# The opening of the forward scans in a convolution-attention, Mamba and expert block: gate projections swapped, state 2 and state 3 prepared in another order

## What is computed

```python
x = x + conv_attention(groupnorm(x))      # keeps the top tenth of each row of scores
t = tokens(x)
t = t + mamba_both_ways(layernorm(t))     # state-space scan, forward and backward
t = t + experts(layernorm(t))             # 8 experts, the best 2 for each token
```

```python
xs, z = split(x @ in_proj_w.T);  xs = silu(causal_conv(xs) + conv_b)
dbc = xs @ x_proj_w.T                     # 16 columns for dt, 16 of B, 16 of C
dt = softplus(dbc[:, :16] @ dt_proj_w.T + dt_proj_b)
h_s[t] = exp(dt[t] * A_s) * h_s[t-1] + dt[t] * B_s[t] * xs[t]    # 16 states s
y = sum over s of h_s * C_s + xs * D;   out = (y * silu(z)) @ out_proj_w.T
```

## Time and profile before

| | us |
|---|---|
| three timed runs: median (lowest to highest) | 1384.38 (1384.08 to 1384.41) |
| profiled execution | 1386.96 |
| its span, first to last instruction | 1385.2 |
| busy: PE, DVE, ACT, POOL | 1246.2, 1136.5, 1000.5, 840.9 |

### The profile page before, as it was taken

The page is one execution under the profiler, slowest core; times in us unless marked ns, Lnnn a source line. Parts: engine busy times, 40 slices in busy tenths (PEclk is TensorE's granted clock), DMA queues, the critical chain, the costliest instruction groups (busy, mean ns, idle before and its releaser), DMA issues. The chain is left out here.

```text
span 1385.2 us, 17997 instructions
## 1 busy us (share of the span) xinstructions
PE 1246.2 (90%) x4857; PEld 675.5 (49%) x4857; DVE 1136.5 (82%) x1352; ACT 1000.5 (72%) x1498; POOL 840.9 (61%) x450
## 2 busy tenths in 40 slices
PE   6249899999988999999989989999998899999969
PEld 2236355554537445455545635545453744545544
DVE  4876799997796689999688679999779668999952
ACT  3826889798755779799755688979865578979923
POOL 3112598797171389889345269879717138988932
PEclk9679899999999989999989979999999999999989
DMA  3000122221030012222021012222103011232203
GB/s 83 16 1 2 49 92 104 89 96 61 16 123 16 33 61 94 106 92 106 1 91 63 3 49 90 106 92 96 56 1 122 16 33 63 91 106 92 107 0 138
DMA packets 30641, 91.91 MB, mean 66 GB/s; under 512 B 4806, under 2 KB 8780, under 8 KB 30572
## 3 DMA queue, kind: packets, MB, share of 16 engines
q1 hardware_dynamic: 27836, 90.03, 18.5%
q10 hardware_dynamic: 2736, 1.08, 0.4%
HBM read 88.34 MB, written 2.75 MB: 66 GB/s over the span
## 5 line engine op out<-in xcount | busy, mean ns | idle before, releaser
L739 POOL TENSOR_TENSOR work<-expo,ring 128x1024 f32<-128x1024 f32 x128 | 300.4, 2368 | 101.2 <-DVE expo L1534 93.0
L739 POOL TENSOR_TENSOR ring<-ring 128x1024 f32<-128x1024 f32 x128 | 301.1, 2373 | 12.0 <-DVE ring L1534 12.0
L1534 DVE TENSOR_TENSOR_SCAN ring<-ring,ps 128x1024 f32<-128x1024 f32 x128 | 284.3, 2262 | 4.0 <-issue 2.1
L1534 DVE TENSOR_TENSOR_SCAN expo<-ring,ps 128x1024 f32<-128x1024 f32 x128 | 285.2, 2270 | 1.8 <-PE ps L1999 1.6
L2036 PE MATMUL ps<-work,ident 128*128 128x512 f32 x512 | 252.0, 598 | 0.8
L2036 PE MATMUL ps<-ring,ident 128*128 128x512 f32 x512 | 246.5, 603 | 3.7 <-POOL ring L739 3.0
L800 ACT ACTIVATE b_dtx_tok<-dtx_tok,b_tok 128x256 f32<-128x256 f32 x448 | 189.3, 493 | 0.0
L1053 ACT ACTIVATE ring<-dt_f,decay 128x1024 f32<-128x1024 f32 x128 | 147.0, 1149 | 42.6 <-DVE expo L1534 24.3
L2036 PEld LDWEIGHTS ps<-ring,ident 128*128 128x128 f32 x512 | 88.7, 190 | 110.9 <-issue 58.5
L1989 PEld LDWEIGHTS ps<-ident,b_dtx_tok 128*128 128x128 f32 x896 | 101.4, 141 | 67.9 <-DVE expo L1534 38.4
L2036 PEld LDWEIGHTS ps<-work,ident 128*128 128x128 f32 x512 | 86.7, 192 | 70.8 <-issue 49.3
(11 more groups left out here) (319 smaller groups left out, 2213.7 us busy)
## 6 DMA issues: line engine op xcount, KB each, us to landing
ring<-c_rows SPq DMA_DIRECT2D x128, 512.0 KB, 3.5
b_dtx_tok<-comb_rows SPq DMA_DIRECT2D x14, 512.0 KB, 4.1
dtx_tok<-comb_rows SPq DMA_DIRECT2D x14, 512.0 KB, 5.6
x_c<-in_x SPq DMA_DIRECT2D x4, 512.0 KB, 3.2
out<-xs_f SPq DMA_DIRECT2D x3, 512.0 KB, 2.6
dt_f<-comb_rows SPq DMA_DIRECT2D x2, 512.0 KB, 7.9
w<-in_L_ffn_w ACTq DMA_DIRECT2D x1, 512.0 KB
w<-in_L_ffn_w SPq DMA_DIRECT2D x1, 512.0 KB
```

The costliest lines, as they stand in the source:

```text
L739: pool.tensor_tensor(hc[odd][:, k, :], hs[odd][:, k, :], c_all[:, odd, :], ALU.mult).then_inc(hc_ready, 1)
L1534: v.tensor_tensor_scan(hs[odd][:, k, order], dA[:, k, order], dbu[:, order], 0.0, ALU.mult, ALU.add).then_inc(scan_ready, 1)
```

## The change

All edits are of order; two idle products are new, and nothing else is computed. On TensorE gate (1,0) is projected before (0,1), with the counts that ScalarE waits for set to match (`z_place`). Ahead of the backward `project_dt`, a wait for three copied token tiles and two idle products into ps01 are added (`keep_busy(2, ps01)`: identity times weights, nothing reads the result). `spread` of state 2 moves ahead of the second backward `project_dt`. In the first pair the turned blocks of state 3 come each before one whole `add` of state 1. On ScalarE three of the eight weightings of state 3 go ahead of B and C of the backward direction, the second decay of state 1 behind them, the two logarithms come together, ahead of the decays of state 2, and `middle_part` goes to the end. On VectorE the products of state 2 stand between the two backward time steps. The backward direction keeps its order.

```diff
+        z_place = ((1, 3), (2, 4))
...
             def z_free(b, d, k):
-                act.wait_ge(z_filled, (b * DIRS + d) * BLOCKS + k + 1)
+                act.wait_ge(z_filled, DIRS * BLOCKS * b + z_place[d][k])
...
                     to_tokens(1)
                     decay_of(1, 0)
-                    decay_of(1, 1)
+                    weigh_by_b(1, range(0, 3))
                     b_and_c(b, 1)
                     top_part(b, 1)
+                    decay_of(1, 1)
                     b_rows(b, 1)
                     dt_log(b, 1, 0)
-                    middle_part(b)
+                    dt_log(b, 1, 1)
                     decay_of(2, 0)
-                    dt_log(b, 1, 1)
-                    weigh_by_b(1, range(0, 4))
                     decay_of(2, 1)
-                    weigh_by_b(1, range(4, TILES))
+                    weigh_by_b(1, range(3, TILES))
                     decay_of(3, 0)
                     weigh_even(2, BY_TOKEN[:2])
                     decay_of(3, 1)
                     weigh_even(2, BY_TOKEN[2:])
+                    middle_part(b)
...
                 products(b, 0, 1, 1, 1)
                 for k in range(BLOCKS):
                     scan_product(b, 0, 1, 1, 1, 1, k, first=True)
+                time_step(b, 1, 0)
+                products(b, 0, 2, 2, 0)
+                time_step(b, 1, 1)
                 for k in range(BLOCKS):
-                    time_step(b, 1, k)
-                later_states(b, 0)
+                    scan_product(b, 0, 2, 0, 2, 0, k)
+                for k in range(BLOCKS):
+                    scan_turned(b, 0, 1, 0, k)
+                more_states(b, 0)
...
+            def next_even(b, d, r, turn):
+                add(b, d, r, 0, [0])
+                spread(b, d, 2 * r + 2, 1 - turn, parts=[0])
+                add(b, d, r, 0, [1], [0])
+                turn_even(b, d, r + 1, 1 - turn, 1)
+                turn_even(b, d, r + 1, 1 - turn, 0)
+                add(b, d, r, 0, [1], [1])
...
                 b_rows(b, 0)
+                project_z(b, 1, 0)
                 project_z(b, 0, 1)
-                project_z(b, 1, 0)
                 dtx_to_tokens(b, 0, 0)
...
                 project_dbc(b, 1, 1)
+                pe.wait_ge(tok_copied, 6 * b + 3)
+                keep_busy(2, ps01)
                 project_dt(b, 1, 0)
                 b_rows(b, 1)
+                spread(b, 0, 2, 0)
                 project_dt(b, 1, 1)
-                spread(b, 0, 2, 0)
                 pe.wait_ge(dt_ready, b * DIRS * BLOCKS + 3)
                 skip_term(0, 0)
                 add(b, 0, 0, 0, [0])
                 pe.wait_ge(dt_ready, b * DIRS * BLOCKS + 4)
                 skip_term(0, 1)
                 add(b, 0, 0, 0, [1])
-                later_states(b, 0, lambda: begin_backward(b))
+                turn_back(b, 0, 1, 0, 0)
+                add(b, 0, 0, 1, [0])
+                turn_back(b, 0, 1, 0, 1)
+                add(b, 0, 0, 1, [1])
+                next_even(b, 0, 1, 0)
+                state_pair(b, 0, 2, 1)
+                with pe.Fori(2, PAIRS // 2) as j:
+                    state_pair(b, 0, 2 * j - 1, 0)
+                    state_pair(b, 0, 2 * j, 1)
+                state_pair(b, 0, PAIRS - 1, 0, lambda: begin_backward(b))
```

More of the change, by code:

```diff
@@ L1565, in gate_last_forward, with state_pair, more_states @@
                                            ALU.mult).then_inc(gated, 1)
-            def state_pair(b, d, r, turn, mixed=True):
-                products(b, d, 2 * r, r + 1, turn, columns=slice(0, BY_TOKEN[0] * P) if mixed else slice(0, N))
+            def state_pair(b, d, r, turn):
+                products(b, d, 2 * r, r + 1, turn, columns=slice(0, BY_TOKEN[0] * P))
                 for k in range(BLOCKS):
-                    (scan_mixed(b, d, r, turn, k) if mixed
-                     else scan_product(b, d, 2 * r, 0, r + 1, turn, k))
+                    scan_mixed(b, d, r, turn, k)
                 for k in range(BLOCKS):
                     scan_turned(b, d, r, turn, k)
-            def later_states(b, d):
-                state_pair(b, d, 1, d, mixed=d == 1)
+            def more_states(b, d):
                 with dve.Fori(1, PAIRS // 2) as j:
@@ L1607, in mamba @@
                     scan_product(b, 1, 1, 1, 1, 0, k)
-                later_states(b, 1)
+                state_pair(b, 1, 1, 1)
+                more_states(b, 1)
             def add_residual(m, projected=ps45):
@@ L2049, in state_pair @@
                 turn_back(b, d, r, turn, 1)
-                add(b, d, r, 0, [0])
                 if then is None:
[L2052 to L2056, removed]
+                    next_even(b, d, r, turn)
                 else:
+                    add(b, d, r, 0, [0])
                     then()
@@ L2073, in backward_states @@
                 add(b, 1, 0, 0, [1], [1])
[L2075 to L2079, removed]
             def begin_backward(b):
@@ L2113, in mamba @@
                 add(b, 0, 0, 0, [1])
-                later_states(b, 0, lambda: begin_backward(b))
+                turn_back(b, 0, 1, 0, 0)
[8 more added lines that the diff above has]
+                state_pair(b, 0, PAIRS - 1, 0, lambda: begin_backward(b))
                 add(b, 0, PAIRS - 1, 1, stop=True)
                 backward_states(b)
-                later_states(b, 1, lambda: None if following is None else queries(following))
+                with pe.Fori(1, PAIRS // 2) as j:
+                    state_pair(b, 1, 2 * j - 1, 1)
+                    state_pair(b, 1, 2 * j, 0)
+                state_pair(b, 1, PAIRS - 1, 1, lambda: None if following is None else queries(following))
             def project_out(m):
```

## The result

| | before | after |
|---|---|---|
| median of nine runs each, on one chip (lowest to highest) | 1384.31 (1379.17 to 1386.34) | 1376.23 (1374.39 to 1377.20) |
| ratio, 95% interval | | 0.9942 (0.9932 to 0.9952) |
| profiled execution; its span | 1386.96; 1385.2 | 1376.84; 1375.0 |

A forecast was written before the change was run, and what follows sets the result against it. The prediction took each image's opening as bound by one chain through three engines, with TensorE's queue the real resource. Four openings 11.5 us shorter gave 1386.96 - 11.5 - 2.58 = 1372.9, say 1373; range 1364 to 1381.

The forecast's parts named there:

- The gate swap: Before VectorE's first products: the 2.36 wait for the first spread shrinks to 0.4, ends 0 and 1.4.
- rival B: Gate swap brings nothing because both gate projections run at half clock; 4 x 1.9 lost, 1380.5; chance 0.12.
- The second fall: TensorE's clock falls again around the backward 17-row projections, rising 3.5 us after dense products start at 165.9.
- TensorE's queue and the give-back: Between state 3's first turn and state 4: whole adds delay state 4's spread and turned tiles, giving back about 1.7 us.
- the step on state 1's decay: Decay behind B and C: VectorE's following work comes 2.3 sooner, ScalarE takes B and C at 157.56 instead of 160.71.
- The idle products: Ahead of the backward dt projections: 1.8 us in a 2.03 wait, pushing the first projection from 158.7 to 159.1.
- the 0.71 becomes 0.3: VectorE's wait for ScalarE's logarithm before the first backward time step shrinks; the step starts 164.6 instead of 167.37.
- forecast opening of 33.86: Time from VectorE's last forward product dt·x to state 4's first scan; four make 135.4 against 146.95.
- Now five us are won, but not all stay: State 3's scan starts 175.8 instead of 180.95; part of that is given back before state 4.
- A: Idle products bridge the wait, so the clock does not fall the second time; openings 31.75, 1364.4; chance 0.17.
- C: Slower: half clock outlasts the skip and add products; openings 38.9, kernel 1393; chance 0.07.
- D: Nothing to measure: TensorE enters state 4 with its queue behind, later pairs wait; 1382 to 1386; chance 0.09.

The follow-up runs named there:

- x2: The changed kernel without the two idle products and the wait before them; 1376.43, ratio 0.9938.
- x5: The changed kernel with half an add between state 3's turned blocks and state 4's spread and turned tiles ahead of the adds; 1377.81, ratio 0.9945.
- x7: The kernel before with the gate projections swapped and nothing else; 1375.66, ratio 0.9932.
- x8: The changed kernel with both backward time steps again ahead of the products of state 2 on VectorE; 1376.81, ratio 0.9939.
- x11: The changed kernel with dt projected on 128 rows in the backward direction alone, forward on 17; 1374.39, ratio 0.9925.
- x1: The changed kernel with the gates projected in the old order; 1382.24, ratio 0.9979.
- x10: The changed kernel with 128-row projections of dt and one idle product instead of two; 1359.94, ratio 0.9836.
- x3: The changed kernel with dt projected on all 128 rows instead of 17, added weight rows zero; 1362.04, ratio 0.9844.
- x6: The changed kernel with 128-row projections of dt, without the two idle products and their wait; 1365.64, ratio 0.9858.
- x4: The kernel before with dt projected on all 128 rows instead of 17; 1378.19, ratio 0.9952.
- x9: The kernel before with the gates swapped, 128-row projections of dt and two idle products, old order of the scans; 1374.03, ratio 0.9928.

## Why the prediction was right, and where it missed

*The gate swap: right, but for one image.* The 2.36 became 0.41 as forecast (0.4) in images 0, 1 and 3. In image 2 all eight gate instructions fell into half clock, as rival B had it, and 2.06 remained. That is 1.65 of the miss. Which image it hits is luck: in the six kernels with the swap and 17-row forward projections (after, x2, x5, x7, x8, x11) a wait of about 2 us stayed in 6 of 24 images, three of them in the one execution of x5.

*The second fall: right.* The clock fell again after the idle products. Dense products started at 164.53 and the clock rose at 168.37: 3.84 us later, 3.5 forecast. The skip and add products so took leg 2 to 8.94 (8.80 forecast).

*TensorE's queue and the give-back: right.* State 4's spread and turned tiles were late by 1.43 and 0.28, 1.7 together, as forecast. Leg 3 is 9.14 (9.10 forecast), and the rest stayed at 145.7 (near 146).

*The term that was mis-sized* is in the step on state 1's decay: "The second half of the backward B/C projection moves from 157.94 to 155.65". Counted from the last product dt·x, with the 0.4 from the gates, that is 5.71; in image 0 it came at 6.09 (154.21 less 148.12). The forecast let TensorE's queue move up by all that VectorE gained, but the last gate's projection now waits 0.36 for ScalarE to copy a gate, which it did not before. The idle products behind it cost what was forecast: the first projection comes at 9.62 with them and at 9.17 without (x2), 0.45 for the 0.4 in the forecast. So "the 0.71 becomes 0.3" fails, the wait is 0.77, and the first time step starts at 15.13 instead of 14.66. Leg 1 is 16.40 in the three images with the short gate wait instead of 15.96; taking the idle products out would not have mended it, since leg 1 of x2 is 15.96 in image 0 and 16.4 to 16.5 in images 1 and 2, where TensorE's queue is late at half clock. The forecast opening of 33.86 so became 34.26 to 34.54, and 36.39 in image 2. Over four images leg 1 makes 3.4 of the 4.2 us by which the openings miss the forecast (67.27 against 4 x 15.96), leg 2 most of the rest.

*A credit that was not there.* "Now five us are won, but not all stay" reads as if a part of state 3's earlier turn stayed. By the forecast's own numbers it does not: legs 2 and 3 are 17.9 there, 17.96 in image 0 before (168.83 to 186.79), and 18.00 measured. The forecast's gain lay in leg 1 (2.4 of the 2.9 us an image, by the table), and x7 and x1 show that there it was the gate swap's.

*The rivals.* A's fall that does not come was not reached by the idle products, but its price was good: x10 holds the clock, with openings of 31.81 (31.75 in A) and 1359.94 (1364.4 in A; the forward dt runs at full clock there too). B happened in one image of four. C did not: the second half clock lasted 6.8 us from 161.5. D did not either: the rest got no longer.

*The Trainium skill* (TensorE: Matmul & The Clock Gate, Part 1: The HAM clock gate) ties the clock to how busy TensorE was of late. The runs agree as far as waits go: with 128-row projections ahead of the skip products the clock fell there in none of the ten images of x3, x6 and x10 where TensorE had idled 1.46 to 1.71, and in nine of the twelve of x4, x6, x9 and x11 where it had idled 1.93 to 2.37. They disagree for products on few rows: in the kernel after the clock fell at 161.54, amid dt projections on 17 rows with the idle products 3.7 us before, and with the same instructions on 128 rows (x3), which take the same time at full clock, it did not fall.

*What stays open.* It is not shown why the clock fell in three images of x9 and x11 and held in the fourth, after the same wait, nor why it fell under the gates in two images of x6, where the rows and waits before are those of the other two. Whether a shorter wait of the skip products (1.71 in x3, 1.47 in x10, 1.93 in x9, 2.15 in x11) would settle the first was not tried.

## What to carry to other kernels

Before an order is changed to close the longest wait, find out whether another engine's queue fills the same time: taking the edits one by one showed a 2 us wait that was the whole gain of the opening and a 3.84 us wait that was worth nothing at half clock. Cut the path into legs between fixed instructions, since a leg that shortens by what the next one grows has moved a wait and not removed it. Where TensorE shows half clock, look at the number of rows of the products ahead of the fall as well as at the waits, and judge an order again after the clock is mended.

## What was not expected of the hardware

Four instructions of dt take 1.88 us on 17 rows or on 128 at full clock, but after the 17-row ones the clock fell to 1.2 GHz in every opening of the kernel after, and after the 128-row ones in none of x3's: 14 us in the median, 11.4 of them in the openings, for weight rows of zeros. Wide rows alone are no warrant: in x4 and x6, without idle products, the clock still fell in some images. And with one program and one wait, 1.93 us in x9, the granted clock was 0.50 in image 2 and 1.00 in image 1; with the old order of the scans that difference was worth 0.05 us.
